# The last product with four plain tiles and fourteen seven-product pairs, its first pair taken from the ring, and the gate's transpose later

## The chip, the cores and the metric

The kernel runs on one core of one Trainium2 chip. The metric is the device time of one execution, in microseconds (us). Execution to execution it differs by some tenths of a per cent.

## What is computed

Input x is 64 batches of 64 channels by 1024. Two layers are added to it:

```python
x = x + _L0_ffn_ref(_L0_cond_ref(x, cond_128, ...), L0_ffn_weight)   # grouped convolution, 8-bit product
x = x + _L1_ffn_ref(_L1_cond_ref(x, cond_128, ...), L1_ffn_W, ...)   # mix of channels, then:
# _L1_ffn_ref(x, W, b, A, Bmat, LiMEs):
H = jnp.einsum('btd,od->bto', x, W) + b
z = jnp.einsum('btd,dr->btr', x, A)
...
probs = jax.nn.softmax(logits, axis=-1)           # the gate, over 8 experts
mask = jax.nn.sigmoid((probs - thresh) / SOFT_TOPK_TEMP)
weights = probs * mask                            # then normalized
p_mix = jnp.einsum('bte,er->btr', weights_full, LiMEs)
delta = jnp.einsum('btr,ro->bto', z * p_mix, Bmat) * scaling
return H + delta
```

H is the last product: 4096 rows by 1024, times a 1024 x 1024 matrix, here in 32 tiles of 128 rows. The change is to how these tiles are worked.

## The kernel before

**Stages.** To about 311 us a loop over the 32 tiles does layer 0 and the mix of layer 1. The rows of the last product (x2) go to a ring of six slots in SBUF, and most of them on to memory (`x2_scratch`). The sum x1, to which the last product is added, goes to memory as well and comes back into one of eight buffers `xb(n)` (slot n modulo 8). From then on the last product runs. Every engine has its order written out by hand, and semaphores join them.

**Plain tiles and pairs.** All float32 factors are split into high and low float16 parts, three matmuls for one. A plain tile (`dense(n, h)`, two halves h) takes 2 x 8 x 3 = 48 matmuls. A pair (`pair(j)`) works two tiles as a 2 x 2 block product with seven products instead of eight: 7 x 4 x 3 = 84 matmuls. It needs sums and differences of the x2 quarters (S parts) and of the W quarters (T parts), each split into high and low.

- T parts, groups q = 0 to 3: ACT scales (`t_scale`), POOL takes four differences (`t_sums`), ACT makes the high parts (`t_high`), POOL the low ones (`t_low`). Group 3 is loaded into the place that group 0 leaves (`x_more`), by SP's `load_t(3)`.
- S parts of pair j: ACT `normalized` and `x_high`, POOL `x_low` and `s_sums` (four operations), ACT `s_high`, POOL `s_low`.
- DVE adds each finished product to `xb(n)`: `fold(n, h)` for plain tiles, `pair_fold(j, i)` for pairs.

**The gate.** PE computes the logits, DVE a chain of small operations, each waiting for the one before (`link`), with two exponentials on ACT in between (L1153, L1155). The last one (L1725) signals `gate_ready`. PE then transposes the gate (L841), ACT copies it (`gateT`), and PE makes `p_mix` from it (`pmix_psum`). DVE multiplies z (`z_mixed`), finds its maxima (`z_max`, `z_top`), scales it (`z_scale`), ACT and DVE split it (`z_high`, `z_low`), and PE adds the low rank update of each tile (`delta(n)`, two matmuls), which DVE adds to `xb(n)` (`add_delta`). Only then can ACT's queue store tile n to `out`, and SP fetch x1 of tile n + 8 into the buffer.

**Order of the tiles.** Before, tiles 26 to 31 are plain (n = 0 to 5), and the pairs are tiles 0 to 25 (n = 6 on), fetched back from memory. Pair j adds the updates of n = 2j + 4 and 2j + 5, and pair 0 those of n = 0 to 5.

**SP's queue** issues in order, behind the loop: the last `save_x1`, the small rows, `fetch_x1(1)` to `(5)`, `load_t(3)`, and then the fetches of x2 and x1. On POOL, before, `t_sums(3)` waits for the gate:

```python
t_low(2)
pool.wait_ge(sem("gate_ready"), 1)
t_sums(3)
x_low(0)
t_low(3)
s_sums(0)
```

Of the kernel before, what the change touches and what calls it, by code (L numbers as in the profile page):

```python
# [39 lines left out]
KEPT = NT - RING  # L40
ORDER = tuple(range(KEPT, NT)) + tuple(range(KEPT))
# [19 lines left out]
def program(nc, x, x_phases, conv_taps, pack, w_nat, w_rows, w_q, mix_w, mix_rows, w_b, b_ffn, out):  # L61
    ctx = ExitStack()
    with ctx:
# [153 lines left out]
        x2_dram = nc.dram_tensor("x2_scratch", [KEPT, P, L], F32, kind="Internal").ap()  # L217
# [66 lines left out]
        def x_tile(j, i):  # L284
            return ring[:, x2_slot(RING + 2 * j + i), :]
# [16 lines left out]
        def _(sp):  # L302
# [101 lines left out]
            def fetch_x2(n):  # L404
                t = ORDER[n]
                if n < 2 * RING:
                    sp.wait_ge(sem("dense_ready"), 2 * (n - RING) + 2)
                else:
                    sp.wait_ge(sem("s_lo_ready"), 2 * ((n - 2 * RING) // 2 + 1))
                sp.wait_ge(sem(f"x2_moved{t % RING}"), 16 * (t // RING + 1))  # L410
                sp.dma_start(ring[:, x2_slot(n), :], x2_dram[t]).then_inc(sem(f"x2_moved{x2_slot(n)}"), 16)

            for c in range(1, NT + 3):
                if c == 3:
                    for t in range(5, SPLIT):
                        load_phases(t)
                if c >= 3 and c + LEAD + 1 < NT:
                    load_phases(c + LEAD + 1)
                if c >= 3:
                    save_x1(c - 3)  # L420
                if c >= 4 and c - 4 < KEPT:
# [48 lines left out]
        def _(pe):  # L470
# [378 lines left out]
            dense(3, 1)  # L849
            dense(4, 0)  # L850
            pe.wait_ge(sem("z_max_ready"), 4)
            tr(ps_small[0:NT, 0:R], z_max[:, :], ident[0:R, 0:R]).then_inc(sem("z_top_psum"), 1)
            dense(4, 1, 0, 4)
            pe.wait_ge(sem("z_top_ready"), 1)
            for i in range(2):
                last = mm(ps_small[:, 128 + i * NT:128 + (i + 1) * NT], z_col4[:, i:i + 1].to_broadcast([NT, P]), ident[0:NT, 0:NT], start=True, stop=True)
            last.then_inc(sem("z_top_psum"), 1)
            dense(4, 1, 4, 8)
# [31 lines left out]
            def pair(j, deltas):  # L890
# [3 lines left out]
                if j == 0:  # L894
                    pe.wait_ge(sem("folded"), 2 * RING - 3)
# [5 lines left out]
                if j == 0:  # L901
                    pe.wait_ge(sem("t_lo_ready"), 8)
                    pe.wait_ge(sem("folded"), 2 * RING - 1)
# [9 lines left out]
                for n in deltas[3]:  # L913
                    delta(n)
                pe.wait_ge(sem("pair_folded"), 7 * j + 3)
                product(sum_a, s_part(j, 1, 0), t_part(0, 1), False)
                for n in deltas[4]:
                    delta(n)
                wait(pe, "pair_folded", 7 * j)
# [6 lines left out]
            dense(5, 0)  # L926
            dense(5, 1)
# [6 lines left out]
        def _(act):  # L934
# [89 lines left out]
            def normalized(n):  # L1024
                t, s = ORDER[n], x2_slot(n)
                act.wait_ge(sem(f"x2_moved{s}"), 16 * (len(range(s, KEPT, RING)) + n // RING))
                act.wait_ge(sem("pair_inv_ready"), 1)
                A(ring[:, s, :], ring[:, s, :], ACT.Copy, scale=pair_inv[:, t:t + 1]).then_inc(sem("norm_ready"), 1)  # L1028
# [127 lines left out]
            t_high(2)  # L1156
            t_scale(3)
# [4 lines left out]
            x_high(0)  # L1162
            t_high(3)
# [6 lines left out]
            def store(n, cols=slice(0, L), parts=7):  # L1170
                if n < RING:
                    act.wait_ge(sem("folded"), 2 * n + 2)
                else:
                    act.wait_ge(sem("pair_folded"), 7 * ((n - RING) // 2) + parts)
# [3 lines left out]
            s_high(0)  # L1178
# [3 lines left out]
            x_high(1)  # L1182
            z_high(1, 0)
            s_high(1)
            store(0)
            store(1)
            normalized(10)
            normalized(11)
            x_high(2)
            store(2)  # L1190
            store(3)
            z_high(2, 1)
            s_high(2)
            store(4)
            store(5)
            for j in range(1, PAIRS):
                if j == 2:
                    z_high(3, 2)
                store(2 * j + 4)
                if j + 2 < PAIRS:  # L1200
                    normalized(2 * j + 10)
                    normalized(2 * j + 11)
                    x_high(j + 2)
                store(2 * j + 5)
# [9 lines left out]
        def _(pool):  # L1214
# [108 lines left out]
        def _(dve):  # L1323
# [344 lines left out]

            rank_out(NT - 6)
# [3 lines left out]
            for t in (NT - 3, NT - 2):  # L1673
                layer0(t + 1, 0)
                layer0(t + 1, 1)
                low(t, 0)
                low(t, 1)
# [3 lines left out]
            dve.wait_ge(sem("t_ready"), 2 * len(BATCHES))  # L1681
            dve.wait_ge(sem("w_scale_ready"), 2)
# [15 lines left out]
            pair_scales()  # L1698
            dve.wait_ge(sem("g_top_psum"), 1)
            v.tensor_reduce(g_top[:, :], ps_small[0:2, 0:P], AX.X, ALU.max).then_inc(sem("gmax_ready"), 1)  # L1700
            fold(1, 0)
            dve.wait_ge(sem("g_top_psum"), 2)
# [23 lines left out]
            fold(1, 1)  # L1726
# [9 lines left out]

            z_mixed(0, 3)
            z_mixed(1, 0)
            z_mixed(2, 1)
            z_mixed(3, 2)  # L1740
            fold(3, 0)
            dve.wait_ge(sem("z_top_psum"), 1)
            link(v.tensor_reduce(z_top[:, :], ps_small[0:NT, 0:R], AX.X, ALU.max))
            link(v.tensor_scalar(z_top[:, :], z_top[:, :], 1e-20, None, ALU.max))
            link(v.tensor_scalar(z_top[:, :].bitcast(U32), z_top[:, :].bitcast(U32), EXPMASK, None, ALU.bitwise_and))
            link(v.tensor_scalar(z_col4[:, 0:1], z_top[:, :], z_unit[0:NT, 1:2], row_floor[0:NT, 1:2], ALU.mult, ALU.max))
            link(v.tensor_scalar(z_col4[:, 2:3].bitcast(I32), z_col4[:, 0:1].bitcast(I32), -1.0, float(254 << 23), ALU.mult, ALU.add))
# [23 lines left out]
            def add_delta(n, folds):  # L1771
                dve.wait_ge(sem("delta_ready"), n + 1)
                if n < RING:
# [7 lines left out]
            def pair_fold(j, i, after=0, deltas=0):  # L1781
                a, b, c = pair_banks(j)
                n1, n2 = RING + 2 * j, RING + 2 * j + 1
# [9 lines left out]

            z_scale(3)
            ends()
            fold(4, 1)
            z_low(0, 3)
            z_scale(0)
            fold(5, 0)
            fold(5, 1)  # L1800
            pair_fold(0, 0)
            add_delta(0, 0)
            add_delta(1, 0)
            pair_fold(0, 1)
            add_delta(2, 0)
            pair_fold(0, 2)
            z_low(1, 0)
            add_delta(3, 0)
            pair_fold(0, 3, after=3)
            add_delta(4, 0)  # L1810
            pair_fold(0, 4, after=2)
            add_delta(5, 0)
            pair_fold(0, 5, after=1)
            z_scale(1)
            pair_fold(0, 6)
            for j in range(1, PAIRS - 1):
                if j == 2:
                    z_scale(2)
                    z_low(2, 1)
                if j == 3:  # L1820
                    z_low(3, 2)
                pair_fold(j, 0)
                add_delta(2 * j + 4, 7 * j)
                pair_fold(j, 1)
                add_delta(2 * j + 5, 7 * j)
                pair_fold(j, 2)
                pair_fold(j, 3, after=3)
# [69 lines left out]
```

## Time and profile before

| | us |
|---|---|
| median of 3 runs | 631.83 (631.68 to 633.12) |
| the profiled execution | 630.61 |
| its span, first to last instruction | 628.8 |
| PE busy | 606.2 |
| DVE, ACT, POOL busy | 413.4, 342.9, 363.8 |
| TensorE clock granted | full, over the whole span |

Busy times overlap. What counts is which engine the others wait for at each place, and that is read from the timeline and the chain that ended last.

### The profile page before, as it was taken

To read this page: it belongs to the slowest core of one execution; us is meant where nothing else is said; L and a number is where in the kernel's file an instruction comes from. 1 tells how busy PE (TensorE), PEld (TensorE's weight loads), DVE (VectorE), ACT (ScalarE), POOL (GpSimd) and SP (SyncE) were. 2 spreads that over 40 slices of the span, in tenths; PEclk is the share of its full clock that TensorE was granted. 3 is DMA by queue.
4 is the path that set the end of the run, shared out by engine and by line. 5 is a ranking of instruction groups with operands and counts; after the bars stand their busy time and mean duration, and the time that the engine had idled before them with its cause. 6 is when DMAs were issued, how large, how long until landed. Compare 5 with 4: busy or idle time off the path is not lost.

```text
span 628.8 us, 15720 instructions
## 1 busy us (share of the span) xinstructions
PE 606.2 (96%) x6268; PEld 341.7 (54%) x6301; DVE 413.4 (66%) x846; ACT 342.9 (55%) x608; POOL 363.8 (58%) x246
## 2 busy tenths in 40 slices
PE   7889999999999999999998999999999999999997
PEld 5556666667666677655553444444444444444443
DVE  7868888977788888887368768564344443344434
ACT  4769999778998888776425253542332331332100
POOL 2325555546776666545395978658765557755400
PEclk9999999999999999999999999999999999999999
DMA  9977988888898888684172317963555434441103
GB/s 348 328 216 270 371 299 295 293 285 298 298 316 310 330 313 313 224 290 143 52 274 71 110 50 268 316 274 104 197 201 201 165 138 147 154 134 68 67 2 133
DMA packets 38342, 136.21 MB, mean 217 GB/s; under 512 B 5004, under 2 KB 5292, under 8 KB 38225
## 3 DMA queue, kind: packets, MB, share of 16 engines
q1 hardware_dynamic: 33518, 118.43, 54.3%
q10 hardware_dynamic: 4752, 16.78, 6.9%
q8 instruction: 50, 0.82, 0.5%
q14 instruction: 22, 0.18, 0.1%
HBM read 87.95 MB, written 47.24 MB: 215 GB/s over the span
## 4 chain that ended last, share of the span: by engine, by line
PE 77%; DVE 6%; issue 2%; ACT 1%; DVEq 0%; ACTq 0%
PE ps L887 37%; PE ps L613 12%; PE ps L688 9%; PE ps L518 7%; PE ps L651 3%; PE ps L597 2%; PE ps L869 2%; DVE yb L1424 2%; PE ps L582 2%; PE ps L625 0%; PE ps L656 0%; PE ps L621 0%; ACT yv L993 0%; PE ps L671 0%; DVE f_all L1459 0%
## 5 line engine op out<-in xcount | busy, mean ns | idle before, releaser
L613 PE MATMUL ps<-wqT,yq_both 128*128 128x512 bf16 x479 | 113.4, 379 | 6.9 <-issue 3.6
L1244 POOL TENSOR_TENSOR x<-x_in,f_all 128x512 f32<-128x512 f32 x64 | 74.1, 1160 | 58.4 <-DVE f_all L1459 57.6
L1248 POOL TENSOR_TENSOR x_split<-x_ph,x_split 128x1032 f16<-128x1032 f32 x25 | 53.7, 2147 | 63.0 <-ACT x_split L966 63.0
L993 ACT ACTIVATE yv<-yb,yinv 128x128 f32<-128x128 f32 x256 | 77.8, 387 | 3.5 <-DVE yinv L1450 3.5
L613 PEld LDWEIGHTS ps<-wqT,yq_both 128*128 128x128 bf16 x512 | 45.4, 97 | 49.9 <-issue 1.5
L1283 POOL TENSOR_TENSOR ring<-ring 128x512 f32<-128x512 f32 x52 | 66.0, 1270 | 4.0
L688 PE MATMUL ps<-ffn_wT,ring 128*128 128x512 f16 x288 | 64.7, 379 | 0.0
L1459 DVE SCALAR_TENSOR_TENSOR f_all<-ps,tok_scale,wsc_b 128x512 f16<-128x512 f32 x64 | 48.0, 749 | 25.1 <-PE ps L613 24.1
L518 PE MATMUL ps<-x_split,conv_h 128*64 128x256 f16 (+1 forms) x1248 | 59.9, 274 | 0.5 <-DVE f_all L1459 0.5
L1028 ACT ACTIVATE ring<-ring,pair_inv 128x1024 f32<-128x1024 f32 x26 | 28.4, 1139 | 53.9 <-DVE x_ph L1779 14.4
L518 PEld LDWEIGHTS ps<-x_split,conv_h 128*64 128x64 f16 (+1 forms) x1248 | 48.6, 108 | 8.9 <-issue 5.2
L1792 DVE SCALAR_TENSOR_TENSOR x_in<-ps,unscale,x_in 128x512 f32<-128x512 f32 x30 | 22.5, 751 | 43.8 <-PE ps L887 43.8
L688 PEld LDWEIGHTS ps<-ffn_wT,ring 128*128 128x128 f16 x288 | 27.4, 98 | 32.2 <-issue 0.8
L1792 DVE SCALAR_TENSOR_TENSOR wst<-ps,unscale,wst 128x512 f32<-128x512 f32 x28 | 21.0, 750 | 36.0 <-PE ps L887 35.9
L966 ACT ACTIVATE x_split<-x_ph 128x1032 f16<-128x1032 f32 x25 | 26.5, 1060 | 27.7 <-PE ps L518 21.5
L1434 DVE TENSOR_REDUCE rowmax<-yb 128x8 f32<-128x1024 f32 x32 | 39.0, 1220 | 1.1
L971 ACT ACTIVATE yq_both<-ps 128x1024 bf16<-128x1024 f16 x32 | 32.6, 1019 | 8.5 <-PE ps L582 8.2
L1424 DVE SCALAR_TENSOR_TENSOR yb<-ps,x_down,ybias 128x1024 f32<-128x1024 f32 x26 | 33.2, 1278 | 6.0 <-PE ps L518 6.0
L1792 DVE SCALAR_TENSOR_TENSOR x<-ps,unscale,x 128x512 f32<-128x512 f32 x21 | 15.8, 751 | 31.5 <-PE ps L887 31.5
L597 PE MATMUL ps<-mix_home,x 64*64 64x64 f32 x2048 | 35.5, 218 | 0.0
L597 PEld LDWEIGHTS ps<-mix_home,x 64*64 64x64 f32 x2048 | 34.1, 135 | 1.3 <-issue 1.1
L983 ACT ACTIVATE ring<-ps 128x512 f32<-128x512 f32 x52 | 27.5, 578 | 1.4 <-PE ps L597 1.4
(343 smaller groups left out, 1195.1 us busy)
## 6 DMA issues: line engine op xcount, KB each, us to landing
x_in<-in_x SPq DMA_DIRECT2D x32, 512.0 KB, 5.8
x_scratch<-x SPq DMA_DIRECT2D x32, 512.0 KB, 3.3
x_ph<-in_x_phases SPq DMA_DIRECT2D x31, 516.0 KB, 5.2
x_scratch<-ring SPq DMA_DIRECT2D x26, 512.0 KB, 4.7
ring<-x_scratch SPq DMA_DIRECT2D x26, 512.0 KB, 4.5
x_in<-x_scratch SPq DMA_DIRECT2D x12, 512.0 KB, 4.4
out<-x_in ACTq DMA_DIRECT2D x12, 512.0 KB, 4.1
wst<-in_w_rows SPq DMA_DIRECT2D x10, 512.0 KB, 6.9
```

The lines of the kernel that those rows point to most:

```text
L518: return mm(ps_conv[o, g * 2 * MB:(g + 1) * 2 * MB], conv_h[k, n, g, w.start + o.start:w.start + o.stop], xp[k, a, g, :, view], start=firs ...
L597: last = mm(bank(2 + e)[j * 64:(j + 1) * 64, k * CH:(k + 1) * CH], x1[b, t % 2, l:l + 64], mixT[b, t, :], start=True, stop=True)
L613: last = mm(acc_bank(t, h), yqT[:, t % 2, p, :], wqT[:, p, h * HALF:(h + 1) * HALF], start=p == 0, stop=p == PH - 1)
L688: last = mm(o, x2_cols[:, x2_slot(n), a, k, :], ffn_wT[:, w, k, h * HALF:(h + 1) * HALF], start=k == 0 and i == 0, stop=k == NL - 1 and i ...
L887: last = mm(b, left(a, k), right(w, k), start=fresh and k == 0 and i == 0, stop=k == 3 and i == 2, skip_group_check=True)
L993: last = A(yv[:, s, :], yb[:, t % 2, s, :], ACT.Copy, scale=yinv[:, s:s + 1], bias=MAGIC)
L1244: g.tensor_tensor(x1[:, t % 2, s], x_in[:, t % 3, s], f16[:, s], ALU.add).then_inc(sem("x1_ready"), 1)
L1248: g.tensor_tensor(x_split[:, (t - SPLIT) % 2, 1, :], phases(t), x_split[:, (t - SPLIT) % 2, 0, :], ALU.subtract).then_inc(sem("xl_ready"), 1)
L1283: g.tensor_tensor(o, x, y, op).then_inc(sem("s_sum_ready"), 1)
L1424: v.scalar_tensor_tensor(yb[:, t % 2, :, :], sets, x_down[:, t:t + 1], bias, ALU.mult, ALU.add).then_inc(sem("yb_ready"), 1)
L1459: v.scalar_tensor_tensor(f16[:, s], acc_bank(t, h), tok_scale[:, t:t + 1], wsc_b[:, s], ALU.mult, ALU.mult).then_inc(sem("f_ready"), 1)
L1792: v.scalar_tensor_tensor(buf, src, unscale[:, t:t + 1], buf, ALU.mult, ALU.add).then_inc(sem("pair_folded"), 1)
```

## The change

Four tiles (28 to 31) are plain. Tiles 26 and 27 are the first pair, taken from the ring where the loop leaves them, in float32 and not split; tiles 0 to 25 are thirteen further pairs. The low rank updates begin in pair 1. The work for z_max and z_top on PE and DVE stands inside pair 0. The gate's transpose stands behind the first half of plain tile 3. The T and S parts are made in another order: POOL's `t_sums(1)` stands inside the loop, `t_low(0)` and `t_low(1)` move to DVE, POOL's wait for the gate is gone, and ACT does all T parts and tile 26's and 27's scaling ahead of the gate's exponentials.

```diff
-KEPT = NT - RING
-ORDER = tuple(range(KEPT, NT)) + tuple(range(KEPT))
+ORD = 4
+KEPT = NT - ORD
+SAVED = NT - RING
+ORDER = tuple(range(KEPT, NT)) + tuple(range(SAVED, KEPT)) + tuple(range(SAVED))
...
-            dense(3, 0, 0, 3)
+            dense(3, 0)
             pe.wait_ge(sem("gate_ready"), 1)
             tr(ps_g[:, 0:P], gate[:, 7, :, :].rearrange("p j e -> p (j e)"), ident[:, :]).then_inc(sem("gateT_psum"), 1)
-            dense(3, 0, 3, 8)
+            dense(3, 1, 0, 3)
...
-            pair(0, ((0, 1), (2,), (3,), (4,), (5,), ()))
-            for j in range(1, PAIRS - 1):
-                pair(j, ((2 * j + 4,), (2 * j + 5,), (), (), (), ()))
+            pair(0, ((), (), (), (), (), ()))
+            pair(1, ((), (), (0,), (1,), (2,), (3,)))
+            for j in range(2, PAIRS - 3):
+                pair(j, ((2 * j,), (2 * j + 1,), (), (), (), ()))
+            for j in range(PAIRS - 3, PAIRS - 1):
+                n = 2 * (PAIRS - 3) + 3 * (j - PAIRS + 3)
+                pair(j, ((n,), (n + 1,), (n + 2,), (), (), ()))
...
@@ act
             high(NT - 2, 1)
+            t_high(1)
+            normalized(4)
+            normalized(5)
+            x_high(0)
             high(NT - 1, 0)
             high(NT - 1, 1)
-            t_high(1)
+            t_high(2)
+            t_scale(3)
+            t_high(3)
             act.wait_ge(sem("gate_in_ready"), 1)
             A(gate[:, 3], gate[:, 2], ACT.Exp).then_inc(sem("gate_exp_ready"), 1)
             act.wait_ge(sem("gate_in_ready"), 2)
             A(gate[:, 5], gate[:, 5], ACT.Exp, scale=-2.0).then_inc(sem("gate_exp_ready"), 1)
-            t_high(2)
-            t_scale(3)
+            s_high(0)
             normalized(6)
             normalized(7)
...
@@ pool
-            t_low(0)
-            t_sums(1)
-            t_low(1)
+                if c + 1 == T_SUMS + 2:
+                    t_sums(1)
             t_sums(2)
+            x_low(0)
+            pool.wait_ge(sem("t_lo_ready"), 4)
             t_low(2)
-            pool.wait_ge(sem("gate_ready"), 1)
             t_sums(3)
-            x_low(0)
+            s_sums(0)
             t_low(3)
-            s_sums(0)
             s_low(0)
...
@@ dve
+            pair_scales()
+            layer0(NT - 2, 0)
+            layer0(NT - 2, 1)
+            low(NT - 3, 0)
+            low(NT - 3, 1)
+            t_low(0)
+            layer0(NT - 1, 0)
+            layer0(NT - 1, 1)
+            low(NT - 2, 0)
+            low(NT - 2, 1)
+            t_low(1)
...
+            add_delta(1, 7)
+            pair_fold(1, 4, after=2)
+            add_delta(2, 7)
             z_scale(0)
-            fold(5, 0)
...
+            pair_fold(1, 5, after=1)
+            add_delta(3, 7)
```

ACT around the gate's two exponentials (`yb<-yb`), before. `mix_home` takes the high T parts of groups 2 and 3, `x_more` is the scaling of group 3:

```order
L1022 ACTIVATE wqT<-row_bias 128x1024 [waits acc_ready,t_sum_ready]
L1022 ACTIVATE wqT<-conv_w 128x1024
L1153 ACTIVATE yb<-yb 128x128 [waits gate_in_ready]
L1155 ACTIVATE yb<-yb 128x128 [waits gate_in_ready]
L1022 ACTIVATE mix_home<-wst 128x1024 [waits mix_ready,t_sum_ready]
L1022 ACTIVATE mix_home<-wst 128x1024
L1011 ACTIVATE x_more<-x_more,w_up 128x1024 [waits t_loaded0]
L1011 ACTIVATE x_more<-x_more,w_up 128x1024
```

The same place in the change:

```order
L1031 ACTIVATE mix_home<-wst 128x1024 [waits mix_ready,t_sum_ready]
L1031 ACTIVATE mix_home<-wst 128x1024
L1020 ACTIVATE x_more<-x_more,w_up 128x1024 [waits t_loaded0]
L1020 ACTIVATE x_more<-x_more,w_up 128x1024
L1031 ACTIVATE mix_home<-x_more 128x1024 [waits mix_ready,t_sum_ready]
L1031 ACTIVATE mix_home<-x_more 128x1024
L1171 ACTIVATE yb<-yb 128x128 [waits gate_in_ready]
L1173 ACTIVATE yb<-yb 128x128 [waits gate_in_ready]
```

Four operations of group 3 and two of group 2 moved ahead of the exponentials.

ACT's first stores to `out`, before (`wqT<-zT` is `z_high`, `wsc_b` and `conv_w` take the S parts of pair 1):

```order
L1168 ACTIVATE wqT<-zT 32x1024 [waits z_scaled]
L1168 ACTIVATE wqT<-zT 32x1024
L1053 ACTIVATE wsc_b<-ring 128x2x512 [waits s_sum_ready,pmix_psum,t_lo_ready]
L1053 ACTIVATE conv_w<-ring 128x2x512 [waits s_sum_ready]
L1176 DMA out<-x_ph 128x1024 [waits delta_added,folded]
L1176 DMA out<-x_in 128x1024 [waits delta_added,folded]
```

And in the change:

```order
L1065 ACTIVATE f_all<-ring 128x2x512 [waits s_sum_ready,prod_ready]
L1065 ACTIVATE yq_both<-ring 128x2x512 [waits s_sum_ready]
L1183 ACTIVATE wqT<-zT 32x1024 [waits z_scaled]
L1183 ACTIVATE wqT<-zT 32x1024
L1191 DMA out<-x_ph 128x1024 [waits delta_added,folded]
L1191 DMA out<-x_in 128x1024 [waits delta_added,folded]
```

The stores now stand behind the S parts of pair 2 and directly behind `z_high(1, 0)`.

## Rows read from the trace of the kernel before

**Rows 1.** The page, busy us (share of the span) and instructions of each engine.

```profile
PE 606.2 (96%) x6268; PEld 341.7 (54%) x6301; DVE 413.4 (66%) x846; ACT 342.9 (55%) x608; POOL 363.8 (58%) x246
```

**Rows 2.** The chain that ended last, 340 to 629 us: start, us, what.

```profile
by line: PE ps L887 81.6%; PE ps L688 10.2%; PE ps L869 4.8%; DVE yb L1721 0.7%; DVE gsm L1723 0.6%; PE ps L847 0.3%; DVE wst L1792 0.3%; PE ps L856 0.2%; PE ps L841 0.1%; DVE yb L1725 0.1%; DVE gsm L1722 0.1%; DVE gsm L1724 0.1%; issue 0.1
...
344.36 3.24 PE ps L688 x15
...
622.09 0.43 PE ps L869 x2
622.52 2.61 PE ps L887 x12
...
625.15 0.75 DVE wst L1792
```

**Rows 3.** The timeline of PE: start, us, line, operation, count [idle before <- releaser].

```profile
332.79 8.59 PE L688 MATMUL ps<-ffn_wT,ring 128*128 128x512 f16 x39
344.03 0.33 PE L841 MATMUL ps<-ident,yb 128*128 128x128 f32 x1 [2.65 <-DVE yb L1725]
```

**Rows 4.** The timeline of ACT, POOL and DVE in the gate, 334 to 344.

```profile
334.91 0.31 ACT L1153 ACTIVATE yb<-yb 128x128 f32<-128x128 f32 x1 [10.53 <-DVE yb L1709]
...
339.06 4.27 POOL L1268 TENSOR_TENSOR mix_home<-wst,mix_home 128x1024 f16<-128x1024 f32 x2 [6.00 <-ACT mix_home L1022]
339.32 2.02 DVE L1721 TENSOR_TENSOR yb<-yb 128x128 f32<-128x128 f32 x1
...
341.70 1.66 DVE L1723 TENSOR_SCALAR gsm<-gsm 128x16 f32<-128x16 f32 x1
...
343.68 0.29 DVE L1725 TENSOR_TENSOR yb<-yb,gsm 128x128 f32<-128x128 f32 x1
```

**Rows 5.** The same timeline, the steps of T parts.

```profile
327.68 5.38 POOL L1263 TENSOR_TENSOR wst<-wst 128x512 f32<-128x512 f32 x4
...
337.95 1.99 ACT L1022 ACTIVATE mix_home<-wst 128x1024 f16<-128x1024 f32 x2
...
339.84 2.17 ACT L1011 ACTIVATE x_more<-x_more,w_up 128x1024 f32<-128x1024 f32 x2
```

**Rows 6.** The same timeline, 303 to 323, and the landing of L385's loads.

```profile
303.70 1.40 DVE L1511 SCALAR_TENSOR_TENSOR ring<-ps,t_up,ring 128x512 f16<-128x512 f32 x2
303.86 1.16 POOL L1244 TENSOR_TENSOR x<-x_in,f_all 128x512 f32<-128x512 f32 x1 [1.02 <-DVE f_all L1459]
...
311.75 1.16 POOL L1244 TENSOR_TENSOR x<-x_in,f_all 128x512 f32<-128x512 f32 x1 [0.57 <-DVE f_all L1459]
...
320.72 1.95 SPq L385 DMA_DIRECT2D x_more<-in_w_rows  x2
...
DMA to landing us min/median/max: 8.2/8.9/9.7
```

**Rows 7.** The timeline of DVE, POOL and ACT, 361 to 372.

```profile
361.99 2.14 POOL L1289 TENSOR_TENSOR f_all<-ring,f_all 128x1024 f16<-128x1024 f32 x1
...
362.75 2.46 DVE L1764 TENSOR_TENSOR zT<-zT,z_both 32x1024 f32<-32x1024 f32 x1
364.07 3.12 POOL L1289 TENSOR_TENSOR yq_both<-ring,yq_both 128x1024 f16<-128x1024 f32 x1
...
369.78 1.21 DVE L1764 TENSOR_TENSOR zT<-zT,z_both 32x1024 f32<-32x1024 f32 x1
...
371.10 2.12 ACT L1168 ACTIVATE wqT<-zT 32x1024 f16<-32x1024 f32 x2
```

**Rows 8.** DVE's timeline at 389, and transfers of 375 to 420: KB, us to landing.

```profile
389.23 1.40 DVE L1779 SCALAR_TENSOR_TENSOR x<-ps,z_both,x 128x512 f32<-128x512 f32 x2
...
out<-x_ph ACTq DMA_DIRECT2D x1, 512.0 KB, 2.7
x_ph<-x_scratch SPq DMA_DIRECT2D x1, 512.0 KB, 4.2
```

More of the change, by code:

```diff
@@ L848, in _, with z_max_out, z_top_out @@
             last.then_inc(sem("pmix_psum"), 1)
[L849 to L858, printed above, removed]
+            dense(3, 1, 3, 8)
+            def z_max_out():
+                pe.wait_ge(sem("z_max_ready"), 4)
+                tr(ps_small[0:NT, 0:R], z_max[:, :], ident[0:R, 0:R]).then_inc(sem("z_top_psum"), 1)
+            def z_top_out():
+                pe.wait_ge(sem("z_top_ready"), 1)
+                for i in range(2):
+                    last = mm(ps_small[:, 128 + i * NT:128 + (i + 1) * NT], z_col4[:, i:i + 1].to_broadcast([NT, P]), ident[0:NT, 0:NT], start=True, stop=True)
+                last.then_inc(sem("z_top_psum"), 1)
             def delta(n):
@@ L1181, in _ @@
             normalized(9)
-            x_high(1)
+            x_high(2)
+            s_high(2)
             z_high(1, 0)
[L1184 to L1195, printed above, removed]
+            stored = 0
             for j in range(1, PAIRS):
                 if j == 2:
+                    z_high(2, 1)
+                if j == 4:
                     z_high(3, 2)
-                store(2 * j + 4)
+                due = (4, 2, 2, 2, 2, 2, 2, 2, 2, 2, 3, 3, 2)[j - 1]
+                for n in range(stored, stored + due // 2):
+                    store(n)
                 if j + 2 < PAIRS:
-                    normalized(2 * j + 10)
-                    normalized(2 * j + 11)
+                    normalized(ORD + 2 * j + 4)
+                    normalized(ORD + 2 * j + 5)
                     x_high(j + 2)
-                store(2 * j + 5)
+                for n in range(stored + due // 2, stored + due):
+                    store(n)
+                stored += due
                 if j + 2 < PAIRS:
@@ L1667, in _, with t_low @@
                     v.tensor_reduce(w_max[:, :], w_part[:, :], AX.X, ALU.max).then_inc(sem("w_max_ready"), 1)
+            def t_low(q):
+                for r in range(2):
+                    dve.wait_ge(sem("t_hi_ready"), 2 * q + r + 1)
+                    v.tensor_tensor(t_home(q)[:, 1, r, :], t_stage(q, r), t_home(q)[:, 0, r, :], ALU.subtract).then_inc(sem("t_lo_ready"), 1)
             rank_out(NT - 6)
@@ L1672, in _ @@
             batch_scale(2)
[L1673 to L1677, printed above, removed]
+            dve.wait_ge(sem("t_ready"), 2 * len(BATCHES))
+            dve.wait_ge(sem("w_scale_ready"), 2)
+            pair_scales()
[9 more added lines that the diff above has]
+            t_low(1)
             low(NT - 1, 0)
@@ L1701, in _ @@
             fold(1, 0)
+            fold(1, 1)
             dve.wait_ge(sem("g_top_psum"), 2)
@@ L1792, in pair_fold @@
                 v.scalar_tensor_tensor(buf, src, unscale[:, t:t + 1], buf, ALU.mult, ALU.add).then_inc(sem("pair_folded"), 1)
+            z_mixed(0, 3)
+            fold(3, 0)
+            z_mixed(1, 0)
+            fold(3, 1)
+            pair_fold(0, 0)
+            z_mixed(2, 1)
+            pair_fold(0, 1)
+            z_mixed(3, 2)
+            pair_fold(0, 2)
+            pair_fold(0, 3, after=3)
+            dve.wait_ge(sem("z_top_psum"), 1)
+            link(v.tensor_reduce(z_top[:, :], ps_small[0:NT, 0:R], AX.X, ALU.max))
@@ L1794, in _ @@
+            link(v.tensor_scalar(z_col4[:, 3:4], z_col4[:, 2:3], w_down[0:NT, 0:1], None, ALU.mult))
+            pair_fold(0, 4, after=2)
+            dve.wait_ge(sem("z_top_psum"), 2)
+            link(v.tensor_scalar(z_both[:, :, :].rearrange("p a t -> p (a t)"), ps_small[:, 128:128 + 2 * NT], 1.0, None, ALU.mult))
             z_scale(3)
             ends()
-            fold(4, 1)
+            pair_fold(0, 5, after=1)
             z_low(0, 3)
-            z_scale(0)
-            fold(5, 0)
@@ L1800, in _ @@
[L1800 to L1816, printed above, removed]
+            pair_fold(0, 6)
@@ new lines, in _ @@
+            pair_fold(1, 0)
+            pair_fold(1, 1)
+            pair_fold(1, 2)
+            add_delta(0, 7)
+            pair_fold(1, 3, after=3)
+            add_delta(1, 7)
+            pair_fold(1, 4, after=2)
+            add_delta(2, 7)
+            z_scale(0)
+            pair_fold(1, 5, after=1)
+            add_delta(3, 7)
+            pair_fold(1, 6)
+            for j in range(2, PAIRS - 1):
+                late = j >= PAIRS - 3
+                n = 2 * min(j, PAIRS - 3) + 3 * max(j - PAIRS + 3, 0)
@@ L1826, in _ @@
                 pair_fold(j, 2)
+                if late:
+                    add_delta(n + 2, 7 * j)
                 pair_fold(j, 3, after=3)
```

75 lines of the change are left out of this document (33 added, 42 removed).

## The prediction

> **What bounds the kernel now.** I read the page first. TensorE (PE) is busy 96% of the span [rows 1], so only two things can move the time: PE work added or removed, and PE waits added or removed. The chain that ended last, from 344 us to the end, is then read [rows 2]. From 344.03 it consists of PE alone until 0.75 us of VectorE (DVE) after the last product. There 12 matmuls take 2.59 to 2.61 us (0.216 us each), and one low rank update takes 0.43 us. So behind the gate's transpose everything on ScalarE (ACT), GpSimd (POOL), DVE and the queues is hidden. The timeline shows the one large wait of the late kernel: PE is idle 2.65 us ahead of that transpose, released by DVE's last gate operation [rows 3]. The softmax gate is thus the hidden chain with the least slack (none), and its inputs are to be followed first.
>
> **Matmuls.** Two plain tiles of 48 go, one pair of seven products of 12 (84) comes: 12 matmuls fewer, 12 x 0.216 = 2.6 us off. The 32 low rank updates are only regrouped. Tile 26's and 27's low parts vanish from DVE (four operations) while PE is waited for anyway; I give that 0, at most 0.5 us off.
>
> **The transpose moved later.** Fifteen matmuls (0.216 each, 3.2 us) now stand ahead of it that stood behind. PE came there at 344.03 - 2.65 = 341.38 and would now come at 344.6; with the gate ready at its old 343.97 it would not wait, and the whole wait of 2.65 would be gone. So the question is when the gate is ready.
>
> **The exponentials on ACT.** Before, ACT ran the gate's first Exp at 334.91, as soon as DVE had its input, and only later scaled and split the last row group of the T parts [rows 4, 5]. Now both Exps stand behind `t_scale(3)` and `t_high(3)` (the first order listing). These need, in series: both loads of the last group landed; scaling on ACT (2.17); POOL's four `t_sums(3)` (5.38 for such four, now placed at once and not held for the gate); ACT's two high parts (1.99) [rows 5]. That is 9.5, with hand-overs 9.7 us after the loads land.
>
> When do they land? The second was issued at about 321.5 and landed 9.7 us later, at 331.2 [rows 6]. The SP queue issues them behind a row: the last save of x1, two small saves, five small loads, five x1 fetches. The head of that row waits for POOL's last addition, which ended at 311.75 + 1.16 = 312.91; the first of the T loads followed 7.8 us later at 320.72 [rows 6]. In the new order POOL does `t_sums(1)` (5.4) ahead of that addition, from about 304.9 (the add at about 303.9 takes 1.16), while DVE does `t_low(0)`, two operations with both inputs in SBUF, from 305.1 [rows 6]. Such operations exclude each other (next part), so the four sums and two subtractions of 1.2 take turns: about 312.4 in place of 310.3. The two additions then end at 314.8, or 316.0 if the first half of DVE's `t_low(1)` gets in between; before it was 312.9. Shift of the loads: 0 if there is no exclusion, up to 3.1; I take 2.4. Landing 333.6, first Exp at 343.3, against 334.91: 8.4 us later.
>
> **DVE against POOL.** In the last group of rows z_scale, a DVE operation with both inputs in SBUF, takes 1.21 alone but 2.46 when POOL works, and POOL's subtraction then takes 3.12 in place of 2.14 [rows 7]. In the gate, the product at 339.32 took 2.02 and a 16-column scaling at 341.70 took 1.66, both ending as a POOL operation of 2.1 ended; a like product takes 0.29 [rows 4], and the scaling's own share I put at 0.2. So each waits for the POOL operation in progress, and they alternate. Only those two were hit before, since POOL stood idle from 333.06 to 339.06 [rows 4, 5], until the high parts came, and its next sums were held until the gate was ready. From the first Exp to the last operation it took 343.97 - 334.91 = 9.06, less 1.73 and 1.46: 5.9 us undisturbed.
>
> Now POOL starts `s_sums(0)` when `t_sums(3)` ends, about 2 us ahead of the Exp, and goes on with `t_low(3)` and `s_low(0)`: 5.3 + 4.2 + 4.3 = 13.8 us without a pause, by the durations in [rows 4, 5, 7]. Behind the Exp, six gate operations have two SBUF inputs or are SBUF scalings. POOL's third sum ends at about 345.2, the fourth at 346.7, `t_low(3)` at 349.0 and 351.3, `s_low(0)` at 353.7 and 356.0 (each pushed a little by DVE). The first product asks at 344.2 and waits 1.0; the top-8 operations (one input, taken as free) bring the second to 346.7, between two, 0; the scaling behind the second Exp asks at 347.4 and waits 1.6; then 1.1 for the next product (350.2 to 351.3), 1.8 for the 16-column scaling, 1.8 for the last product: 7.3 in all. Where one slips in between two of POOL's, something comes off. I take 6.5. The bounds are 0 (POOL does not interfere) and 9 (each of the six waits out most of an operation). Gate ready: 343.3 + 5.9 + 6.5 = 355.7, against 343.97: 11.7 later. PE comes at 344.6 and waits 11 us, where it waited 2.65. Behind PE's wait nothing else can go: all products are in order on PE.
>
> The Trainium skill (SBUF — State Buffer, section Who interferes with whom) says that DVE instructions with two SBUF inputs, and scalings in a two-port mode, are locked out for the whole of a GpSimd instruction that reads SBUF, and reductions never are. By that rule the six wait as walked. With no rule at all, the two rows alone would say 1.6 us each, 9.6 in all.
>
> **The first pair's own needs.** Its tiles 26 and 27 are scaled in the ring from 314.6; its sums' parts are due 9 us after the transpose and ready by about then. z_max and z_top work is interleaved with its folds, with PE coming within a us of each. I cost this at 0, up to 1.5: the cover is the products of 2.6 us between.
>
> **The second pair and the stores.** The updates for tiles n = 0 to 3 now stand in pair 1, and the same eight buffers must serve n = 8 already in pair 2; before there was one more pair between. On ACT the stores of n = 0 and 1 stand behind `z_high(1, 0)`, which waits for DVE's `z_scale(0)`, which stands behind the third update (the second order listing). From pair 1's start on PE: five products and three updates, 14.2; fold and update on DVE (0.75 and 1.40) to 16.1; z_scale 1.2 to 2.5; two high parts 2.12; the store lands in 2.7, the fetch in 4.2; the fold 0.75 [rows 2, 7, 8]. That is 27.7 to 29.0. PE needs it at 7 x 2.59 + 4 x 0.43 + 2 x 2.59 + 2 x 0.43 = 25.9. A new wait of 1.8 to 3.1; I take 2.5. From pair 3 on a buffer has two pairs (38 us) for store and fetch, about 17 us of work: 0.
>
> **Sum.** 11.7 (gate) - 3.2 (matmuls moved ahead of the transpose) - 2.6 (matmuls gone) + 2.5 (stores) = +8.4 us. The profiled execution took 630.61 with a span of 628.8, so its like is 639.0 and 637.2. The median of the three runs, 631.83, is 1.2 above it; I forecast 640.2.
>
> **Rivals.**
> - *Exps late, but POOL hardly interferes or the loads aren't shifted.* For it: the walk hangs on who asks first at each of POOL's ends. Against: three measured waits of 1.2 to 1.7 [rows 4, 7]. Terms: 6.5 down to 2, or the shift 2.4 to 0: +3 to +5, 635 to 637.
> - *The other side: the Exps are not late.* If the loads landed early enough that `t_high(3)` is through by 336, the gate is ready by 344.6 and PE doesn't wait; -2.65 - 2.6, and the stores' 0 to 2.5: 626.6 to 629. It decides where landing + 9.7 is under 335, a landing by 325. The row says 331.2, and nothing in the change issues them sooner. Close to it, with no shift and no interference at all: gate at 341.0 + 5.9 = 346.9, PE waits 2.3, and 2.9 - 3.2 - 2.6 + 2.1 = -0.8, 631.0.
> - *The pairs do not keep pace.* Stores and fetches one pair tighter cost PE a us or more in each pair: 645 to 655. Against: 17 us of work in 38.
> - *The change does what it says and nothing else*, 12 matmuls and the wait: 626.6, that of the second rival.
>
> **Numbers.** Anything under 0.3% (1.9 us) can't be told from no change here. Forecast (637.5 to 643.5): 0.63. First rival (634 to 637.5): 0.18. About no change: 0.07. Faster: 0.08. Pairs too slow: 0.04. So slower 0.85, same 0.07, faster 0.08. The range takes in the first rival and most of the bounds of the forecast: 632.5 to 644.5.
>
> **What would show it.** PE's wait ahead of the gate's transpose: 9 to 13 us, released by DVE. ACT's first Exp right behind the two high parts of the last group, at 342 to 345. The gate's small DVE operations at 1 to 2 us each instead of 0.3. The T loads issued 2 to 3 us later. A wait of about 2.5 us in the third product of pair 2, released by a fold that waited for a fetch. I am wrong if the Exp runs before 338, or if PE's wait there is under 4 us.

## The result and the profile after

| | before | after |
|---|---|---|
| median, us | 631.75 (631.49 to 633.12, 4 runs) | 640.01 (635.62 to 642.01, 4 runs) |
| the profiled execution | 630.61 | 639.47 |
| its span | 628.8 | 637.7 |
| PE busy | 606.2 | 609.6 |
| TensorE clock granted, mean | 1.00 | 0.992 |

The ratio is 1.0112, with a 95% interval of 1.007 to 1.0154: the change makes the kernel slower by 8 us (4.4 to 9.7 by the interval), and 640.2 was forecast. A second measurement, experiment 7, whose edit turned out to move nothing, gave a ratio of 1.0083, which is 5.3 us.

PE's timeline around the gate's transpose, in the trace after. It answers to [rows 3]:

```profile
334.55 11.83 PE L690 MATMUL ps<-ffn_wT,ring 128*128 128x512 f16 x54
355.93 0.48 PE L843 MATMUL ps<-ident,yb 128*128 128x128 f32 x1 [9.56 <-DVE yb L1747]
356.20 4.05 PE L690 MATMUL ps<-ffn_wT,ring 128*128 128x512 f16 x9
```

PE is idle for 9.56 us, released by the gate's last DVE operation. Everything it waits for from 290 us to the end, as the view of waits groups it (us in total, times, longest):

```profile
PE ps L843 <- DVE yb L1747: 9.6, 1, 9.6
PE ps L615 <- issue: 0.2, 1, 0.2
```

There is no other wait. The steps ahead of the exponentials, which answer to [rows 5, 6], in the timeline of ACT, POOL and SP's queue:

```profile
313.72 2.28 POOL L1256 TENSOR_TENSOR x<-x_in,f_all 128x512 f32<-128x512 f32 x2
...
323.15 1.87 SPq L387 DMA_DIRECT2D x_more<-in_w_rows  x2
...
333.99 2.19 ACT L1020 ACTIVATE x_more<-x_more,w_up 128x1024 f32<-128x1024 f32 x2 [8.83 <-DMA x_more<-in_w_rows]
...
336.25 5.29 POOL L1275 TENSOR_TENSOR x_more<-x_more 128x512 f32<-128x512 f32 x4 [5.77 <-ACT x_more L1020]
...
341.58 2.00 ACT L1031 ACTIVATE mix_home<-x_more 128x1024 f16<-128x1024 f32 x2 [5.40 <-POOL x_more L1275]
343.49 0.29 ACT L1171 ACTIVATE yb<-yb 128x128 f32<-128x128 f32 x1
```

POOL's last addition ends at 316.0 (312.9 before), the T loads are issued at 323.15 (320.72 before), and then scaling, four sums and two high parts run in series, with the first Exp at their end. The gate itself, behind the first Exp, DVE and POOL ([rows 4] before):

```profile
344.43 1.20 DVE L1735 TENSOR_TENSOR yb<-yb,gsm 128x128 f32<-128x128 f32 x1
345.65 1.19 DVE L1737 MAX8 yv<-yb 128x8 f32<-128x8 f32 x16
346.77 4.25 POOL L1280 TENSOR_TENSOR mix_home<-x_more,mix_home 128x1024 f16<-128x1024 f32 x2
346.88 2.17 DVE L1739 TENSOR_TENSOR yb<-yb,yv 128x128 f32<-128x128 f32 x1
...
349.42 1.69 DVE L1741 TENSOR_SCALAR yb<-yb 128x128 f32<-128x128 f32 x1 [0.38 <-ACT yb L1173]
...
351.14 0.95 DVE L1742 RECIPROCAL yb<-yb 128x128 f32<-128x128 f32 x1
...
352.13 1.12 DVE L1743 TENSOR_TENSOR yb<-yb 128x128 f32<-128x128 f32 x1
353.07 2.17 POOL L1301 TENSOR_TENSOR yq_both<-ring,yq_both 128x1024 f16<-128x1024 f32 x1
...
353.61 1.65 DVE L1745 TENSOR_SCALAR gsm<-gsm 128x16 f32<-128x16 f32 x1
...
355.59 0.29 DVE L1747 TENSOR_TENSOR yb<-yb,gsm 128x128 f32<-128x128 f32 x1
```

The products and scalings take 1.1 to 2.2 us where they take 0.2 to 0.3 undisturbed, and each ends within 0.2 us of the end of one of POOL's operations; MAX8 (1.19) and the reciprocal (0.95) take what they took before. Only the last product takes 0.29: POOL had nothing to do from 355.24 on.

One thing in this trace was not in the prediction. In windows of 2 us (busy time and instructions of each engine, then PE's granted clock):

```profile
348.00:350.00 2.00, 0.00 (x0) 0.00 (x0) 1.62 (x2) 0.92 (x2) 2.00 (x2) 1.00 0.00 0
350.00:352.00 2.00, 0.00 (x0) 0.00 (x0) 1.97 (x2) 2.00 (x3) 2.00 (x2) 0.75 0.00 0
352.00:354.00 2.00, 0.00 (x0) 0.00 (x0) 1.90 (x4) 1.36 (x2) 2.00 (x2) 0.50 0.00 0
...
358.00:360.00 2.00, 2.00 (x6) 0.52 (x4) 0.00 (x0) 0.19 (x1) 2.00 (x2) 0.50 0.00 0
360.00:362.00 2.00, 2.00 (x35) 1.38 (x35) 0.18 (x1) 0.00 (x0) 1.84 (x3) 0.69 0.00 0
362.00:364.00 2.00, 2.00 (x11) 0.89 (x10) 1.97 (x2) 0.64 (x1) 1.92 (x2) 1.00 0.00 0
```

While PE is idle its granted clock falls from 1.00 (2.4 GHz) to 0.50 (1.2 GHz), and it is back only at about 361. So the nine matmuls behind the transpose take 4.05 us instead of 2.10.

**Where the 8.9 us of span went.** The transpose starts at 355.93 instead of 344.03: +11.9. From it to the end of the last product it is 278.1 us (355.93 to 634.0) instead of 281.1 (344.03 to 625.1): -3.0. Of the 11.9, some 1.8 was there before the gate came into it: the operation that feeds the last addition, the same in both programs, starts at 312.68 against 310.92. Experiment 8 shows that this much comes and goes from one execution to the next. So what the change itself costs in this trace is nearer 7.1 us than 8.9.

### The profile page after: what moved, and what is told of

It is laid out like the page before. It is cut to its first block, busy times and chain, and to the rows that moved or that the text cites. A ratio compares the mean times of both kernels' runs of the same rounds, so it can differ in the third digit from the quotient of the medians.

```text
span 637.7 us, 15709 instructions
## 1 busy us (share of the span) xinstructions
PE 609.6 (96%) x6256; PEld 343.5 (54%) x6289; DVE 423.3 (66%) x847; ACT 348.2 (55%) x614; POOL 370.5 (58%) x250
## 4 chain that ended last, share of the span: by engine, by line
PE 70%; DVE 6%; issue 3%; POOL 2%; DMA 2%; ACT 1%; SPq 1%; DVEq 0%; POOLq 0%; ACTq 0%
PE ps L890 39%; PE ps L615 11%; PE ps L520 7%; PE ps L653 3%; PE ps L872 2%; DVE yb L1435 2%; PE ps L690 2%; PE ps L599 2%; DMA x_more<-in_w_rows 2%; PE ps L584 1%; POOL x_more L1275 1%; POOL x L1256 1%; POOL row_bias L1275 1%; PE ps L627 1%; POOL conv_w L1275 0%
## 5 line engine op out<-in xcount | busy, mean ns | idle before, releaser
L1295 POOL TENSOR_TENSOR ring<-ring 128x512 f32<-128x512 f32 x56 | 71.1, 1269 | 4.3
L1040 ACT ACTIVATE ring<-ring,pair_inv 128x1024 f32<-128x1024 f32 x28 | 30.6, 1139 | 42.4 <-DVE x L1782 13.1
L690 PE MATMUL ps<-ffn_wT,ring 128*128 128x512 f16 x192 | 45.5, 391 | 0.0
L975 ACT ACTIVATE x_split<-x_ph 128x1032 f16<-128x1032 f32 x25 | 26.5, 1060 | 27.7 <-PE ps L520 21.5
L1795 DVE SCALAR_TENSOR_TENSOR x<-ps,unscale,x 128x512 f32<-128x512 f32 x28 | 20.9, 747 | 30.6 <-PE ps L890 29.7
L992 ACT ACTIVATE ring<-ps 128x512 f32<-128x512 f32 x56 | 29.7, 579 | 2.2 <-PE ps L599 2.1
L690 PEld LDWEIGHTS ps<-ffn_wT,ring 128*128 128x128 f16 x192 | 18.5, 100 | 22.6 <-issue 2.9
```

Source lines behind the costliest of these rows:

```text
L690: last = mm(o, x2_cols[:, x2_slot(n), a, k, :], ffn_wT[:, w, k, h * HALF:(h + 1) * HALF], start=k == 0 and i == 0, stop=k == NL - 1 and i ...
L1295: g.tensor_tensor(o, x, y, op).then_inc(sem("s_sum_ready"), 1)
L1795: v.scalar_tensor_tensor(buf, src, unscale[:, t:t + 1], buf, ALU.mult, ALU.add).then_inc(sem("pair_folded"), 1)
```

## The experiments

My theory was that of the prediction: the gate is late for two reasons that add up, the exponentials' place behind the last T group, whose loads come late, and POOL's operations in the gate, which lock DVE out. The rivals were that one of the two carries all, or that the pairs or the stores cost something of their own. The first four kernels ran together (before there: 633.12, 630.63 to 634.78, 20 runs), and the last four on another occasion (before: 633.17, 631.66 to 635.41, 13 runs). The kernel before was 1.4 us slower on both than in the result (631.75), so kernels of different occasions are compared by their ratios to it. All edits but the last are to the changed kernel.

**1. POOL held until the gate is ready**, behind the last T sums. `s_sums(0)` and all behind it wait:

```diff
             t_sums(3)
+            pool.wait_ge(sem("gate_ready"), 1)
             s_sums(0)
```

> The changed kernel, but POOL waits for the gate before its first S sums (s_sums(0)), so it stands idle while DVE works behind the first Exp. My theory (DVE's operations wait out POOL's): from the first Exp to the last gate operation 5.9 us instead of 12.4, PE's wait ahead of the transpose 3 us instead of 9.6; then POOL's 13.8 us of work starts at the gate and the first pair's second product, due 8.9 us behind the transpose, waits about 5 us. Time 636 to 638 (the changed kernel 640.0). Rival (DVE is slowed by something else, POOL has no part): the stretch stays 12.4, the wait of 5 us comes on top, 645.

Measured: 637.36 (636.35 to 639.24), ratio 1.0075 (1.0051 to 1.0099). First Exp at 342.33, transpose at 348.21: the gate takes the 5.9 us undisturbed that the prediction had, against 12.4. Its 16-column scaling, and then PE's two large waits in this trace:

```profile
347.37 0.17 DVE L1746 TENSOR_SCALAR gsm<-gsm 128x16 f32<-128x16 f32 x1
...
348.21 0.33 PE L843 MATMUL ps<-ident,yb 128*128 128x128 f32 x1 [2.94 <-DVE yb L1748]
...
356.60 0.26 ACT L1178 ACTIVATE wsc_b<-ps 128x128 f32<-128x128 f32 x1
...
356.91 1.93 PE L849 MATMUL ps<-wsc_b,limes_n 32*32 32x128 f32 x32 [6.42 <-ACT wsc_b L1178]
```

The lock is worth 6.6 us, and nearly all of it is given back at once: ACT's copy of the gate stands behind `s_high(0)`, whose sums POOL now makes late, and PE waits 6.42 us for the copy. Another 2.0 us of PE's waits stand at two folds (0.4 and 1.6), where the changed kernel has none. The time came out as expected, but the wait is at another place than I had put it, and by its time alone this kernel can't be told from the changed one (the intervals overlap). What shows the lock is the trace.

**2. The last T group loaded early**: SP issues the loads inside the loop, ahead of the last save of x1.

```diff
+                if c == NT + 1:
+                    load_t(3)
...
-            load_t(3)
```

> The changed kernel, but SP issues the last two T loads ahead of the last save of x1, the small rows and the x1 fetches. My theory (the first Exp is late because the T work of group 3 stands ahead of it on ACT and that waits for these loads): they land by about 318, ACT's scaling follows t_high(2) at once, POOL's four differences end by 336, the first Exp runs at about 338 instead of 343.5, the gate is ready 4 to 6 us earlier, PE's wait falls from 9.6 to 3 to 5 us. Time 631.5 to 635. Rival (POOL's work and the lock set the gate wherever the Exp stands): the stretch behind the Exp grows by what the Exp gains, 638 to 640.

Measured: 633.10 (631.76 to 634.64), ratio 1.0005 (0.9988 to 1.0022). ACT's timeline:

```profile
324.04 2.17 ACT L1021 ACTIVATE x_more<-x_more,w_up 128x1024 f32<-128x1024 f32 x2
334.83 2.00 ACT L1032 ACTIVATE mix_home<-x_more 128x1024 f16<-128x1024 f32 x2 [8.61 <-POOL x_more L1276]
338.90 0.31 ACT L1172 ACTIVATE yb<-yb 128x128 f32<-128x128 f32 x1 [2.07 <-DVE yb L1732]
```

The T steps are through by 336.8 and the Exp waits for DVE instead, 4.6 us earlier than in the changed kernel. PE still waits 3.9 us at the transpose. Loading early is thus enough to make up the whole loss against the kernel before. The 3.9 us that remain I put down to the lock: from the Exp to the transpose it is 10.4 us, where it is 5.9 undisturbed. Experiment 4 takes this away as well.

**3. The exponentials ahead of the T steps on ACT**, and the gate's copy ahead of `t_high(3)`, with the loads as late as in the change:

```diff
-            t_scale(3)
-            t_high(3)
             act.wait_ge(sem("gate_in_ready"), 1)
...
+            t_scale(3)
+            act.wait_ge(sem("gateT_psum"), 1)
+            A(gateT, bank(2)[:, 0:P], ACT.Copy).then_inc(sem("gateT_ready"), 1)
+            t_high(3)
             s_high(0)
```

> The changed kernel, but ACT runs the two Exps right behind t_high(2), then t_scale(3), the gate's copy, t_high(3), s_high(0). My theory: first Exp at about 337, gate ready before PE comes at 346.4, its wait there 0 to 1 us. The T and S parts are then late: POOL has 19 us of work from about 342 on, the first pair's second product waits about 6 us. Time 633 to 636. Rival (the gate was late for another reason than its place on ACT): the wait stays at the transpose, 640 or more.

Measured: 635.01 (633.32 to 635.86), ratio 1.0026 (1.0011 to 1.0041). The Exp runs at 335.37 and PE does not wait at the transpose (344.92). But what the T steps are needed for is now late itself, the second product of pair 0:

```profile
359.62 1.46 PE L890 MATMUL ps<-x_ph,f_all 128*128 128x512 f16 x3 [5.55 <-POOL yq_both L1301]
```

So the gate's new place on ACT cannot be undone alone. It is not the late loads by themselves that are waited for here: `t_scale(3)`, now behind both Exps, starts at 338.40, where in experiment 1, a kernel with the same late loads, it starts at 332.83. The gate and the T steps are needed close behind each other (at 344.9 and at 354.1 here), and whichever stands second on ACT is waited for.

**4. Both**: the loads early, and POOL held for the gate, but only behind `s_sums(0)`, so that ACT's copy of the gate does not come late.

```diff
+                if c == NT + 1:
+                    load_t(3)
...
             s_sums(0)
+            pool.wait_ge(sem("gate_ready"), 1)
             t_low(3)
```

> The T loads early as in the second run, and POOL waits for the gate between s_sums(0) and t_low(3). Both causes go: first Exp at about 338, POOL's sums end at about 341, the rest of the gate undisturbed, gate ready at 346 to 347, PE's wait 0 to 1; t_low(3) and s_low(0) (8.5 us) end at about 355.5, when the second product of pair 0 is due. Time 627.5 to 630, under the kernel before (631.8). Rival (one of the two causes alone held all of it): no better than the best of the first two runs.

Measured: 627.45 (627.16 to 629.92), ratio 0.993 (0.9902 to 0.9957). This version beats both kernels. Ahead of the Exp (340.59) POOL still holds DVE up (0.8 to 1.4 us for operations of 0.3). DVE's gate, which from 340.9 on runs undisturbed, and the transpose:

```profile
343.16 0.29 DVE L1741 TENSOR_TENSOR yb<-yb,yv 128x128 f32<-128x128 f32 x1
...
345.08 0.29 DVE L1745 TENSOR_TENSOR yb<-yb 128x128 f32<-128x128 f32 x1
...
346.22 0.29 DVE L1749 TENSOR_TENSOR yb<-yb,gsm 128x128 f32<-128x128 f32 x1
...
346.92 0.27 PE L844 MATMUL ps<-ident,yb 128*128 128x128 f32 x1
```

No wait stands at the transpose. What is left is 2.0 us at two folds, in pairs 2 and 4 (0.2 and 1.8). The rival, that it would be no better than the better of 1 and 2, fell.

**5 and 6. PE kept busy while it waits.** 38 or 20 matmuls whose results nothing uses stand in the 9.6 us of idle time. The clock is thus changed with all else as it was:

```diff
             dense(3, 0)
+            for _ in range(38):
+                mm(bank(3), ffn_wT[:, 0, 0, 0:P], ffn_wT[:, 0, 0, 0:HALF], start=True, stop=True)
             pe.wait_ge(sem("gate_ready"), 1)
```

> The changed kernel with 38 extra matmuls of 512 columns between plain tile 3's first half and the wait for the gate; their results are used by nothing. 38 x 0.216 = 8.2 us, inside the 9.6 us for which TensorE waits there in the changed kernel, so by themselves they cost nothing. Theory A (the fall of the granted clock to 0.50 behind the wait costs about 2.4 us): the remaining wait of 1 to 1.5 us leaves the clock at full, the nine matmuls behind the transpose take 0.216 each and not 0.43, and the time falls by 2 to 3 us: 636.5 to 638.5 against a before of 631.8 to 633, ratio 1.007 to 1.009. Theory B (the clock's fall costs nothing, since the engines around it set the pace there): no change against the changed kernel, ratio 1.011.

> As the last one, with 20 extra matmuls (4.3 us), so that a wait of about 5.2 us is left. A wait of 2.7 to 2.9 us was seen with no fall, waits of 5.6 and 6.4 us with a fall to 0.50. If the length of the idle stretch alone decides, the fall is there, perhaps shorter, and the time is that of the changed kernel less 0 to 1.5 us: ratio 1.009 to 1.011. If the fall wants the whole 9.6 us, it is gone and the ratio is 1.007 to 1.009.

Measured with 38: 637.26 (636.67 to 638.02), ratio 1.0063 (1.0048 to 1.0078), mean clock 1.0. With 20: 637.92 (637.83 to 640.0), ratio 1.0081 (1.0063 to 1.0099), clock 0.992. PE with 38, and then with 20:

```profile
355.55 0.33 PE L845 MATMUL ps<-ident,yb 128*128 128x128 f32 x1 [1.08 <-DVE yb L1749]
355.71 2.10 PE L690 MATMUL ps<-ffn_wT,ring 128*128 128x512 f16 x9
```

```profile
354.22 0.48 PE L845 MATMUL ps<-ident,yb 128*128 128x128 f32 x1 [4.89 <-DVE yb L1749]
354.48 4.05 PE L690 MATMUL ps<-ffn_wT,ring 128*128 128x512 f16 x9
```

From the transpose to the end of the last product it is 275.5 us with 38 matmuls, 278.3 with 20, 278.1 in the changed kernel. So the fall of the clock costs 2.5 us on PE's path here, and a wait of 4.9 us brings as much (2.7). It is not a fixed price, though: in experiment 7, after a wait of 8.7 us, the same nine matmuls took 3.70, and transpose to last product is 277.2, 1.7 more than with 38:

```profile
355.88 3.70 PE L690 MATMUL ps<-ffn_wT,ring 128*128 128x512 f16 x9
```

By the traces the cost is shown; by the times alone it is not, since the intervals of 5 and 6 overlap. Against experiment 7, measured with them, the 38 matmuls gain 1.3 us, with intervals that overlap too. The ratio of 5 is below the 1.007 to 1.009 that I expected, and that of 6 lies in the range I gave to the theory that its trace refutes.

**7. The first stores issued later**, behind four operations of ACT instead of two:

```diff
-                for n in range(stored, stored + due // 2):
-                    store(n)
+                if j > 1:
+                    for n in range(stored, stored + due // 2):
+                        store(n)
...
                     normalized(ORD + 2 * j + 5)
+                    if j == 1:
+                        store(0)
+                        store(1)
```

> The changed kernel with the first two stores issued behind the scaling of tiles 10 and 11 in the program of ScalarE instead of ahead of it. In the changed kernel the first store was issued at 401.26, while the first of two high parts of z was still running and before the second began, and the fold that needs the buffer ended 1.8 us before TensorE wanted it. Theory A (a DMA is issued when the queue comes to it, without waiting for the operations ahead to end, but not ahead of their start by more than one): issue at about 403.4 to 404.5, 2.1 to 3.2 us later, fetch and fold as much later, and TensorE waits 0.3 to 1.4 us in pair 2's third product; time within 0.2% of the changed kernel. Theory B (it waits for the operations ahead to end, as the prediction assumed): issue at 405.6 or later, 4.3 us later, TensorE waits 2.5 us or more.

Measured: 638.51 (637.7 to 639.53), ratio 1.0083 (1.0068 to 1.0098), and a trace that refutes both of my theories:

```profile
400.03 1.06 ACT L1183 ACTIVATE wqT<-zT 32x1024 f16<-32x1024 f32 x1 [5.84 <-DVE zT L1771]
...
400.27 0.38 ACTq L1191 DMA_DIRECT2D out<-x_ph  x1
...
401.11 1.06 ACT L1183 ACTIVATE wqT<-zT 32x1024 f16<-32x1024 f32 x1
...
402.19 2.19 ACT L1040 ACTIVATE ring<-ring,pair_inv 128x1024 f32<-128x1024 f32 x2
```

The store is issued 0.24 us after the first of four operations that all stand ahead of it in the program has begun, as early as in the changed kernel (0.06). The edit moves nothing. As its time should be that of the changed kernel, it is also a second measurement of it, within the first one's interval: 5.3 us over the kernel before (4.3 to 6.2).

The trace of the kernel before shows the same thing, and the prediction missed it. The high parts of pair 1 stand ahead of the first store there, and the store is issued at 380.29, before the second of them ends at 380.59:

```profile
379.53 1.06 ACT L1053 ACTIVATE conv_w<-ring 128x1024 f16<-128x1024 f32 x1 [1.56 <-POOL ring L1283]
380.29 0.38 ACTq L1176 DMA_DIRECT2D out<-x_ph  x1
```

**8. One part of the change alone, on the kernel before**: the transpose 15 matmuls later.

```diff
-            dense(3, 0, 0, 3)
+            dense(3, 0)
             pe.wait_ge(sem("gate_ready"), 1)
...
-            dense(3, 0, 3, 8)
+            dense(3, 1, 0, 3)
```

> The kernel before with one part of the change alone: the gate's transpose behind the whole first half of plain tile 3 and three eighths of the second, 15 matmuls later. The gate is ready at 343.97 as before and TensorE comes at 344.6, so it does not wait; 2.65 us go: ratio 0.996 (629.2 against 631.8, or 630.5 against 633.1). Rival: what hangs on the transpose (z's maxima and the first low rank updates in pair 0) is then late by 0.6 us and is waited for again, so nothing or only part is won: ratio 0.998 to 1.0. Together with the version that loads early and holds GpSimd (ratio 0.993) it says what the twelve matmuls less are worth: that ratio less this one, forecast 0.004.

Measured: 631.50 (631.0 to 632.1), ratio 0.9972 (0.9959 to 0.9985). PE's waits from 290 us on:

```profile
PE ps L852 <- DVE z_max L1734: 1.2, 1, 1.2
PE ps L613 <- issue: 0.2, 1, 0.2
PE ps L613 <- DVE yb L1424: 0.2, 1, 0.2
```

The 2.65 us at the transpose are gone, and 1.2 of them come back at z's maxima, which hang on it: between the theory and its rival. This ratio less experiment 4's is 0.0042, or 2.7 us, as the twelve matmuls (2.6) would have it, though the two intervals leave about 2 us either way. With the waits of each taken off, the two traces say the same: transpose to last product is 275.5 us in 4 and 278.1 in 8.

This trace also settles the shift ahead of the gate. The program is the same as before up to 340 us, and yet the operation that feeds the last addition starts at 313.63, 2.7 us later than in the trace before, and the first Exp is later by the same 2.7 (337.61). So the 1.8 us of the changed kernel's trace cannot be told from what one execution differs from the next, and the next section takes it off.

## Why the prediction was right

- **The exponentials on ACT.** First Exp forecast at 343.3, measured at 343.49, behind the two high parts. The mechanism is right, and the agreement is luck. Of the 8.6 us by which the Exp is later, 1.8 is the shift of the whole trace; 6.8 is left, where 8.4 was forecast (6.0 to 6.8 in the five traces with the loads and the Exp as in the change). The term that was too large is the shift of the loads, 2.4: they are issued 2.4 later, but 1.8 of it is the trace's, so their own shift is 0.7. The additions end 1.3 later by themselves (3.1 less 1.8), since the T sums alternate with DVE's `t_low(0)` (4.52 for two operations that I priced at 1.2 each), and SP's row from there to the T loads took 0.7 less than before.
- **DVE against POOL.** 6.5 us of waiting forecast, 6.6 measured: 0.9, 1.9, 1.5, 0.8, 1.5 and 0. Single terms of the walk missed (the second product I had at 0, the last at 1.8), and the sum held, since each wait is what is left of a POOL operation of 1.3 to 2.1. Experiment 1 takes the lock away and finds the 5.9 us that were worked out as undisturbed. The Trainium skill (SBUF — State Buffer, section Who interferes with whom) has the lock last the whole instruction, with the reductions free of it. The trace agrees: the reductions at 343.82 and 353.29, both beside a running POOL operation, take 0.29.
- **PE's wait.** 11 forecast, 9.6 measured. The gate is ready at 355.88, as forecast (355.7), but PE came at 346.4, where I had 344.6. The difference is the 1.8 us by which the whole trace is late. The gate is late by it too, and there it hid that the loads' own shift was 1.7 less than forecast.
- **Matmuls.** The 12 gone and the 15 moved, 5.8 us together, stood as forecast: 281.1 - 5.8 = 275.3, and 275.5 with the clock held up (experiment 5).
- **The step that failed: the stores.** "A new wait of 1.8 to 3.1; I take 2.5" measured 0. I had the store wait for both high parts of z to end, and it was issued beside the first one, at 401.26, where 403.3 was forecast by that rule:

```profile
401.20 1.06 ACT L1183 ACTIVATE wqT<-zT 32x1024 f16<-32x1024 f32 x1 [5.85 <-DVE zT L1767]
401.26 0.38 ACTq L1191 DMA_DIRECT2D out<-x_ph  x1
...
407.40 0.75 DVE L1795 SCALAR_TENSOR_TENSOR x_ph<-ps,unscale,x_ph 128x512 f32<-128x512 f32 x1
...
409.88 0.81 PE L890 MATMUL ps<-x_ph,yq_both 128*128 128x512 f16 x3
```

  The fold that needs the buffer ended at 408.15, and PE's third product of pair 2 began at 409.88 without a wait. From pair 1's start (383.96) that is 24.2 us where the prediction had 27.7 to 29.0. The listed terms themselves add up to 27.1 to 28.4, a slip of 0.6. From 27.1, with z_scale at the low end as measured (1.20), the issue takes 2.0 off and the fetch, landed in 3.3 and not 4.2, 0.9 more. With the high parts waited for, PE would still have waited only some 0.3. The Trainium skill (Advanced Engine Details and Errata, section Engine Queue Depths) gives ScalarE a queue of 8 instructions; the four that the issue overtakes in experiment 7 are within it. The slack is thin all the same: in experiment 4 the fetch for n = 9 comes late enough for 0.2 us of PE's wait.
- **The term that was missing: the clock.** +2.5, which no row of before could show, since in its trace a wait of 2.65 us left the clock at 1.00. It filled the place of the stores' term almost to the tenth.

The sum of +8.4 thus holds two errors of 2.5 that cancel and one of 1.6, the Exp's lateness, that the shift of the trace covered: without the shift the trace says +7.1, and the second measurement +5.3. Right was the mechanism at the gate and its two large terms in kind; the agreement of 640.0 with 640.2 is better than the working deserves. Of the first rival (635 to 637), little interference fell with the rows of DVE, but its other half, no shift of the loads, came nearer than my 2.4, and the second measurement lies at its edge. Pairs that do not keep pace fell with the list of waits.

## What to carry to other kernels

When instructions are put in another order on one engine, follow the shortest hidden chain (here a gate of small operations) through every queue that it now shares, and look at what else runs beside it: the order that cost 5 to 8 us here costs nothing once one group's loads are issued earlier and one engine is held back for some 5 us, and the kernel is then 0.7% faster than before. A wait that is taken away early must be followed to the next one, since in experiments 1, 3 and 8 nearly half or more of it came back at the next semaphore of the same chain. Price a long wait of TensorE at its own length and the slow matmuls behind it (1.6 to 2.7 us here, behind waits of 3.9 to 9.6). And before a time of two traces is put down to a change, look how far apart the traces already are ahead of it.

## What was not expected of the hardware

- **The clock and the idle stretch.** Idle stretches of 3.9, 4.9, 5.6, 6.4, 8.7 and 9.6 us each had matmuls at 0.50 of full clock (1.2 GHz) behind them, those of 1.1, 2.65 and 2.9 us none. The cost did not follow the length. From the transpose to the last product it was, over the 275.5 of experiment 5, 1.6 us after 3.9 (experiment 2, where the clock fell only with the matmuls running again), 2.7 after 4.9, 1.7 after 8.7 and 2.5 after 9.6. Matmuls that nobody needs, put into the idle time, kept the clock up in the trace. What is open: 11 of the 33 executions of the kernel before on the two later occasions had a mean clock of 0.992 to 0.997, the two at 0.992 with times of 634.7 and 634.8, 1.6 us above the median. No trace of them was kept, so where their clock fell is not shown.
- **DMAs issued from ACT's queue pass operations that stand ahead of them.** In experiment 7 the issue comes before four of them have ended, and before three of them have begun. Whether more than four can be passed no run here shows.
- **The same instructions start up to 2.7 us apart at 311 us** from one execution to the next: 310.92 and 313.63 in the two traces of the kernel before's program, and 311.31 to 313.21 in six traces whose program up to there is that of the change. A shift of that size ahead of the place of a change need not be an effect of it.
